# Long attention: VectorE normalises a pair's short row before the maximum of a later long row

## The reference, cut to what matters

```python
# xn: (2, 1024, 128), 8 heads in 2 groups of 4, head size 128
q = (x @ wq).reshape(Bq, Tq, N_KV, N_REP, HEAD_DIM)
k_lat = (x @ wk_down).reshape(Bq, Tq, N_KV, D_LAT)
v_lat = (x @ wv_down).reshape(Bq, Tq, N_KV, D_LAT)
k = jnp.einsum('bkhl,ld->bkhd', k_lat, wk_up)
v = jnp.einsum('bkhl,ld->bkhd', v_lat, wv_up)
scores = jnp.einsum('bqhrd,bkhd->bhrqk', q, k) * scale
scores = jnp.where(causal, scores, jnp.finfo(scores.dtype).min)
probs = jax.nn.softmax(scores, axis=-1)
y = jnp.einsum('bhrqk,bkhd->bqhrd', probs, v)
return y.reshape(Bq, Tq, N_HEADS * HEAD_DIM) @ wo
```

## Time and profile before

| what | value |
|---|---|
| median of 3 runs | 1997.72 us (1994.52 to 2001.73) |
| profiled execution, its own time | 1988.82 us |
| its span | 1987.0 us |
| busy in the span: PE, DVE, ACT, POOL | 1824.3, 1503.3, 1331.3, 1400.2 us |
| attention rounds | from 33 to 346 us of the span |
| second round (117.59 to 197.06): PE, DVE, ACT, POOL busy | 65.32, 55.60, 52.59, 24.31 us |
| granted TensorE clock, mean | 0.986 |

### The profile page before, as it was taken

How to read it: one execution, slowest core, us unless ns; L and a number is a source line. 1 busy time by engine, 2 the same in 40 slices (tenths; PEclk the granted TensorE clock), 3 DMA queues, 4 the chain that set the end, 5 groups by cost and what they waited for, 6 DMA issues and landing times.

```text
span 1987.0 us, 70561 instructions
## 1 busy us (share of the span) xinstructions
PE 1824.3 (92%) x29444; PEld 1296.0 (65%) x29444; DVE 1503.3 (76%) x2286; ACT 1331.3 (67%) x2154; POOL 1400.2 (70%) x1494
## 2 busy tenths in 40 slices
PE   5878788689999999999999999999999999999995
PEld 4656666456667666666666666666766666667664
DVE  4866868477887888878878878878787788887862
ACT  5766766355776677667766776677767766776664
POOL 2322334588888778888778977888877888877771
PEclk9999999799999999999999999999999999999998
DMA  3000000200001000010000000000100000000000
GB/s 109 2 1 0 0 1 1 74 3 2 3 2 47 3 2 14 3 47 3 2 14 3 23 26 3 14 2 2 47 3 2 14 2 3 3 2 2 8 2 17
DMA packets 12463, 25.52 MB, mean 13 GB/s; under 512 B 1856, under 2 KB 9728, under 8 KB 10496
## 3 DMA queue, kind: packets, MB, share of 16 engines
q1 hardware_dynamic: 12160, 21.18, 3.2%
HBM read 20.13 MB, written 1.05 MB: 11 GB/s over the span
## 4 chain that ended last, share of the span: by engine, by line
PE 73%; ACT 10%; DVE 8%; issue 7%; POOL 1%; DMA 1%; ACTq 0%; DVEq 0%; SPq 0%; POOLq 0%
PE banks L1089 30%; PE banks L1311 15%; PE banks L1245 10%; PE banks L1335 8%; PE banks L1297 5%; DVE small L894 3%; PE banks L1172 2%; PE banks L1286 2%; ACT L783 2%; ACT arena L679 1%; ACT arena L783 1%; ACT L786 1%; DVE arena L948 1%; DVE banks L889 1%; DVE arena L883 1%
## 5 line engine op out<-in xcount | busy, mean ns | idle before, releaser
L1311 PE MATMUL banks<-M,xs 128*32 128x512 f32 x3072 | 368.6, 596 | 0.5 <-ACT arena L719 0.2
L458 POOL TENSOR_TENSOR arena<-arena 128x1024 f32<-128x1024 f32 x96 | 229.8, 2394 | 165.6 <-DVE arena L948 165.6
L719 ACT ACTIVATE arena<-banks 128x1024 f32<-128x1024 f32 x192 | 197.2, 1027 | 121.2 <-PE banks L1311 120.1
L995 DVE TENSOR_REDUCE small<-banks 128x16 f32<-128x1024 f32 x96 | 117.5, 1224 | 200.7 <-PE banks L1297 200.7
L943 DVE TENSOR_TENSOR arena<-banks,tabs 128x1024 f32<-128x1024 f32 x192 | 233.3, 1215 | 45.8 <-ACT arena L679 38.5
L948 DVE TENSOR_TENSOR arena<-banks,tabs 128x1024 f32<-128x1024 f32 x192 | 232.8, 1212 | 0.0
L463 POOL TENSOR_TENSOR arena<-arena 128x1024 f32<-128x1024 f32 x96 | 229.0, 2385 | 0.0
L1335 PE MATMUL banks<-arena 128*32 128x128 f32 x6144 | 189.7, 276 | 15.9 <-DVE arena L1039 15.6
L1245 PE MATMUL banks<-cst,arena 128*128 128x128 f32 x1536 | 200.7, 274 | 0.0
L1245 PEld LDWEIGHTS banks<-cst,arena 128*128 128x128 f32 x1536 | 177.3, 141 | 22.6 <-issue 2.5
L453 POOL TENSOR_TENSOR prob<-prob,small 128x1024 f32<-128x1024 f32 x96 | 184.0, 1917 | 10.4 <-DVE small L985 10.4
(11 more groups left out here) (127 smaller groups left out, 4156.7 us busy)
## 6 DMA issues: line engine op xcount, KB each, us to landing
qkraw<-in_wqk_dram SPq DMA_DIRECT2D x6, 1024.0 KB, 4.7
arena<-in_wvo_dram SPq DMA_DIRECT2D x6, 1024.0 KB, 4.7
W<-in_w_dram SPq DMA_DIRECT2D x6, 341.0 KB, 3.3
W<-in_w_dram SPq DMA_DIRECT2D x6, 192.0 KB, 2.4
res<-in_x_dram SPq DMA_DIRECT2D x4, 256.0 KB, 3.7
tabc<-in_tab_dram SPq DMA_DIRECT2D x1, 1024.0 KB, 7.2
out_dram<-res SPq DMA_DIRECT2D x4, 256.0 KB, 3.0
sca_s<-in_sca_dram SPq DMA_DIRECT2D x6, 128.0 KB, 4.8
```

The source lines that it names most:

```text
L458: pool.tensor_tensor(kc, kc, ks, ALU.add).then_inc(s["k_add"], 1)
L719: act.activation(vw[:, (2 * k + g) % RV, :], two(V_BANK), ACT.Copy).then_inc(s[f"v_cp{g}"], 1)
L1311: ins = pe.matmul(bk(V_BANK + z)[WIN * q:WIN * (q + 1), :], xs[:, b, t0:t0 + WIN], M[:, q, :, :].rearrange("p m n -> p (m n)"), start=True ...
```

## The change

In VectorE's queue the bodies are now written out two at a time. For a pair (j, j + 1) the normalising of the short row j + 1 is put directly behind its reciprocal, and ahead of the maximum of the long row j + 4 and of the sum that is due there. All instructions and all other engines' orders stay.

```diff
-                for j in range(len(bodies)):
+                for j in range(0, len(bodies), 2):
                     normalise(j)
                     if ahead(j) is not None:
                         cap(ahead(j))
-                    if j < LAST:
-                        inverse(j + 1)
+                    inverse(j + 1)
+                    normalise(j + 1)
                     if ahead(j) is not None:
                         peak(ahead(j))
                     for i in due(j, 2, 3):
+                        add_out(it, i)
+                    if ahead(j + 1) is not None:
+                        cap(ahead(j + 1))
+                    if j + 1 < LAST:
+                        inverse(j + 2)
+                    if ahead(j + 1) is not None:
+                        peak(ahead(j + 1))
+                    for i in due(j + 1, 2, 3):
                         add_out(it, i)
```

## The result

The changed kernel took 2004.46 us, the median of 11 runs (2001.18 to 2007.92), against 1998.01 us for the kernel before beside it (11 runs, 1993.90 to 2001.73). The ratio is 1.0036, 95% interval 1.0026 to 1.0046: some 7 us slower (6.5 between the medians), and more than the 3.8 us that were forecast.

What follows compares the result with a forecast made beforehand. VectorE, idle only 0.38 us a pair, was taken to bound the attention loop, with ScalarE's exponentials next. Four rounds of +1.2 us less 1.0 gave +3.8: 1992.6 us profiled, 2001.5 us as median; range 1989 to 2009.

Steps and rivals of the forecast that it cites:

- a case with a chance of 0.37: Whole kernel: the outcome slower, given 0.37 beside faster 0.15 and same 0.48; about 6 us counted as no change.
- stage 1: First four pairs of a round: scaled maxima mostly come earlier, long outputs start 0.4 us earlier; -0.4 us a round at best.
- first pairs of stages 2, 3, 4: Pairs where TensorE waits for the sum: the short normalising now comes first, losing 0.34, 0.41 and 0.49 us; +1.2 a round.
- other pairs of stage 2: Stage 2 behind its first pair: 0.45 and up to 0.27 us less, last long row's transposes 0.26 later; together -0.5 a round.
- stages 3 and 4, other pairs: Pairs there without a sum: 0.09 us more VectorE work each and a ScalarE loop no shorter; +0.2 us a round.
- GpSimd collisions: Moved normalising can hit the second part of GpSimd's split, waiting up to 0.27 us in 9 of 14 pairs; +0.7 a round.
- last round: Early normalisings escape GpSimd's 1.27 us instructions, which begin about 1.1 us behind the mask; -1.0 us once, bounds 0 to -2.8.
- the loop over ScalarE: First-stage pairs: maximum, long and short exponentials, reciprocal, normalising become the new loop, 3.36 us against 3.57 at 896 columns.
- the waits of the reciprocal (L878) for the short exponential: Sign to look for in the profile after: VectorE's reciprocal waits for ScalarE's short exponential grow to over 10 us.
- rival 2: GpSimd's split blocks normalisings in most pairs, 0.27 us in 11 pairs a round; 2011 us, chance 0.25.
- The first: TensorE's wait was the bound: ScalarE has slack, some 0.4 us less in 6 pairs a round; 1989 us, chance 0.15.
- The third: Change doesn't reach the time: first-pair losses hide behind TensorE's outputs as the gains do; 1998 us, chance 0.2.

Runs made afterwards that it cites:

- e1: Kernel before, with the short row's normalising moved early only in the four pairs of each round's first stage; 1999.62 us, ratio 1.0001.
- e2: Kernel before, with the normalising moved early only in the three pairs where a sum is due; 2006.57 us, ratio 1.0037.
- e9: Changed kernel with 8 idle matmuls a round on TensorE, ahead of the transposes of body 28; 1993.78 us, ratio 0.9967 to the kernel before.
- e11: Kernel before with 3 and 3 idle matmuls near each round's end and 4 more in the last round; 1987.60 us, ratio 0.9925.
- e6: Changed kernel with ScalarE's exponential of the short row put ahead of its evacuation; 2002.11 us, ratio 1.0016 to the kernel before.
- e5: Kernel before with 3 idle matmuls ahead of the transposes of body 27 and 3 ahead of body 28's; 1991.66 us, ratio 0.9957.
- e7: Kernel before with ScalarE's exponential of the short row put ahead of its evacuation; 2001.88 us, ratio 1.0005.
- e4: Changed kernel with 14 idle matmuls a round on TensorE, ahead of the transposes of body 28; 1995.09 us, ratio 0.9975 to the kernel before.
- c_before: Kernel before, unchanged, run once more for a second profile; 2005.42 us in its one run.
- e3: Kernel before, with the normalising moved early in stages 1 to 3 except the pairs with a sum; 2000.26 us, ratio 1.0002.

## Why the prediction was right, and where it was not

The forecast was 2001.5 us; it came to 2004.46, inside the range of 1989 to 2009. It is slower, like the sum; at 1.0036 it lies just past the 0.3% that were called no change, a case with a chance of 0.37. On the profiled attention the sum said +3.8 us and 7.6 came. Step by step, for a looped round:

| step | predicted | measured | shown by |
|---|---|---|---|
| stage 1 | -0.4 | -0.13 | e1 |
| first pairs of stages 2, 3, 4 | +0.34, +0.41, +0.49 | +0.30, +0.38, +0.68 | e2 |
| other pairs of stage 2 | -0.45, -0.27, +0.26 | -0.47, -0.34, +0.27 | after |
| stages 3 and 4, other pairs | +0.2 | +0.07 in stage 3, some +0.2 in stage 4 | after; e9 against e11 |
| GpSimd collisions | +0.7 | in the rows above | after, e6 |
| half clock | none | +1.0, where before had kept the clock | e9, e5 |
| last round | -1.0 beside the +1.2 | +4.2 in all | after, e6 |

**The mechanism held.** The wait of the earlier trace rows went, the loop over ScalarE took its place within the same pair (3.48 us where 3.36 and a collision were reckoned), and the pairs with a sum lost what the normalising takes. With the clock kept on both sides (e9 against e11), the rounds differ by 0.86, 0.95 and 0.89 us, and the sum had said 1.2. That it came so near is in part luck: stage 1 was put 0.3 too low, and the collisions 0.5 or more too high. The total came into a range 20 us wide with the clock left out and the last round wrong in sign. One sign was read wrong: the waits of the reciprocal (L878) for the short exponential were to grow to over 10 us and are 5.6. The loop closes at another of its corners: VectorE is so full behind the long maximum that it mostly reaches the reciprocal when the exponential is done, and the time shows as ScalarE's wait for L896 (16.3 to 35.2 us) instead.

**Stage 1 was mis-sized.** The pairs ran ahead by 0.53 us as the walk had it, but 0.46 came back in the passage. It is of a kind with the last pairs of stages 2 and 3 (+0.27, +0.19), where TensorE waits for a long row whose normalising now comes later; the walk had this for stage 2 and left it out for stage 1. The traces show it: TensorE began the transposes of the stage's last long row 0.20 us ahead of the mask before (135.28 against 135.48), and 0.22 behind it after (135.62 against 135.40), having waited 0.58 us for L883; the long outputs behind them start 0.47 us later from the mask. No run tried this alone.

**The collisions were mis-sized, though their place was right.** I added new ones and did not take away the old. The short normalisings by form, changed kernel, 33 to 352 us (times, busy us, mean ns, then idle before):

```profile
L883 DVE TENSOR_SCALAR arena<-arena,small 128x512 f32<-128x512 f32 x16 | 8.5, 533 | 0.6
L883 DVE TENSOR_SCALAR arena<-arena,small 128x256 f32<-128x256 f32 x16 | 8.1, 508 | 0.6
L883 DVE TENSOR_SCALAR arena<-arena,small 128x384 f32<-128x384 f32 x16 | 7.2, 448 | 0.6
L883 DVE TENSOR_SCALAR arena<-arena,small 128x128 f32<-128x128 f32 x16 | 6.0, 378 | 0.6
```

Before they were, in the same order, 491, 566, 486 and 277 ns on average. The sums are 29.8 and 29.2 us: 0.6 us more in four rounds, where 2.8 were reckoned. 128 and 512 columns got slower, 256 and 384 faster. In the first pair of stage 4 the new collision lies on the path (0.62 us where 0.49 were reckoned), 0.13 of the 0.19 us by which that pair missed its forecast. The rest is a term read from another pair: the forecast took off 0.12 or 0.13 us between reciprocal and maximum, and in this pair they were 0.08 apart (173.82 and 173.90). The reciprocal starts 0.45 us behind the mask, held by ScalarE; it did so before (0.44), so this is no part of the difference, but e6 gives 0.38 us back there, and e7 0.16.

**The last round failed, in sign.** An early normalising was to slip in before GpSimd's long instructions. VectorE and GpSimd in the last round of the changed kernel:

```profile
311.15 0.28 DVE L889 TENSOR_TENSOR banks<-banks,cst 128x128 f32<-128x128 f32 x1
311.62 1.28 POOL L400 TENSOR_TENSOR xsL<-xs,xsH 128x512 fp32r<-128x512 f32 x1
311.67 1.37 DVE L883 TENSOR_SCALAR arena<-arena,small 128x256 f32<-128x256 f32 x1
```

The split of the shifted input starts 0.47 us behind the mask, not 1.1 as in the earlier trace rows: with TensorE ahead of VectorE, GpSimd's queue is ahead too. The normalising follows it by 0.05 us and takes 1.37 us, more than the 1.15 of before. This is the mechanism of rival 2, met where its price is highest; stage 2 of the last round lost 0.77 us, 0.28 of them in this pair. The Trainium skill ("SBUF — State Buffer", Who interferes with whom) says that of VectorE in a two-port mode and GpSimd the one that issues first keeps the other out, and these rows agree with it, in both directions: in stage 1 GpSimd's L386 took 0.96 us, not 0.40, when a normalising had begun 0.04 us earlier.

**The missing term is the clock.** In the changed kernel a stretch of half clock costs about 1.0 us in each looped round (81.44, 81.39 and 80.85 us against 80.36, 80.40 and 79.75 in e9). Since before had it in two of the three, the difference is only some 1.0 us there. The last round's fourth column is 3.18 us longer. Of these 2.26 lie behind the start of the last long outputs, where only the clock differs (8.11 against 5.85 us; e4, at full clock, has 5.69), and 0.92 ahead of it. The order of VectorE thus costs the last round 1.97 us (0.21, 0.77, 0.07 and 0.92 in its four columns). Of the 8.0 us by which the four rounds grew some 4.7 are the order and some 3.3 the clock.

Whether the clock's share belongs to the change is shown for the looped rounds more than for the last. Of the 18 looped rounds in the six profiles with idle matmuls none has a half clock. Of the 18 in the six profiles without them and without the early order in stage 4's last pairs (before, c_before, e1, e2, e3, e7) 9 have one, and of the 6 in the changed kernel and e6 it is 5. In the last round it falls with the new order (after, e9) and with the old (c_before, e5), and it stays away with the new (e4, e6) and with the old (e7): there one profile of the changed kernel can't tell the change from chance.

**The rivals.** The first, that the wait of 25.7 us was the bound, is refuted: it went and the time rose. The second was right on one pair of the last round and wrong as a rule for all. The third, that losses and gains hide, is refuted by e2: three pairs' loss reached the round whole (1.36 us of pairs, 1.35 of round 2), and the time rose clear of its interval.

**What stays open.** e4 is 9 us faster than the changed kernel (12 by the ratios), while its attention part is only 1.7 us shorter. It is so with all six kernels with idle matmuls: e5 and e11 are 8.8 and 13.6 us faster than before, with a last sum only 0.3 and 2.6 us earlier. Most of what idle matmuls gain therefore does not lie where they stand, and was not found. Behind the attention the layers have places where the clock falls. I count windows of some 30 us around five of them with a clock under 1: with idle matmuls in the attention 0, 1, 2, 0, 0 and 0 in six profiles, and 1633.0 to 1640.5 us from the last sum to the end (1637 on average); without them 1 to 4 in eight profiles, and 1635.8 to 1652.2 us (1646 on average). The count goes with the time, but the two sets overlap, and why work at the end of the attention should bear on a layer hundreds of us later was not found. One profile of each kernel is too little to call it shown. By the same token, that the 6.5 us between the medians are the 7.6 of the attention rests on e2, which repeats both the loss and the time, and on the two numbers being near each other.

## What to carry to other kernels

Hold a long wait in the list against the idle time of the engine that is waited for; here 25.7 us stood against 0.38 us of VectorE's idle time a pair, and the wait moved to what now stands behind. Before an instruction is moved forward in an in-order queue, name the first instruction that it passes and who waits for that: here the sum (L872), in 3 pairs of 16, made most of the order's loss. And where two short waits of TensorE become one long one, look at the granted clock of the stretch behind it.

## What the runs showed of the hardware

One wait of TensorE of 2.20 us was followed by matmuls at 1.2 GHz (1.05 us for four that take 0.66) in every looped round of the changed kernel. In its last round a wait of 2.04 us was not: the four took 0.63 us, and the clock fell 5 us later. Two waits of 0.9 us with 0.65 us of work between were followed by it in some rounds and executions of the same kernel and not in others. Six idle matmuls a round, of 0.12 us a pass and two passes each, kept the clock in the looped rounds (e5, e11), four more kept it in the last (e11). These kernels, whose arithmetic is untouched, took 0.4 and 0.75% less time, as much as the change in question cost or more, though most of that gain was not traced to these rounds.

The clock also fell where TensorE had hardly waited. At the end of a layer, at 746 us of the changed kernel, TensorE makes 12 matmuls of one column (TensorE in time):

```profile
745.54 0.34 PE L1305 MATMUL banks<-arena 64*32 64x64 f32 x14 [0.59 <-issue]
746.03 1.33 PE L1097 MATMUL banks<-parv,W 128*128 128x1 f32 x12
...
747.66 0.63 PE L1097 MATMUL banks<-qkL,xsH 128*128 128x512 f32 x1
```

In e9 the same 12 are followed by the same matmul at 0.39 us, at a granted clock of 1.00: the fall comes in one execution and not in the other. The two differ in what went before, too: the idle 0.59 us at 745 us are not there in e9. Whether that wait made the difference isn't shown.
